# Expert outputs added into four sums in DRAM by POOL's scatter, in place of a pick per token and expert

## The reference, cut to what matters

```python
router_logits = x @ gate_w
probs = jax.nn.softmax(router_logits, axis=-1)
top_vals, top_idx = jax.lax.top_k(probs, 8)
top_vals = top_vals / jnp.sum(top_vals, axis=-1, keepdims=True)
rw = jnp.zeros((T, 64)).at[jnp.arange(T)[:, None], top_idx].set(top_vals)
h = silu(x @ w_gate[e]) * (x @ w_up[e]) * rw[:, e]     # for each expert e
out = sum over e of h @ w_down[e]
x = x + tanh(g_ffn[1]) * out                           # x is normalised before the experts
```

## Time and profile before

| what | value |
|---|---|
| median of three runs | 416.84 us (415.79 to 417.10) |
| the profiled execution | 417.87 us |
| its span | 416.1 us |
| mean granted TensorE clock | 0.844 |
| PE / PEld busy | 275.1 / 230.9 us |
| DVE / ACT / POOL busy | 210.7 / 118.0 / 214.0 us |
| bytes moved by DMA | 84.12 MB |

### The profile page before, as it was taken

The page is one execution under the profiler, slowest core; times in us unless marked ns, Lnnn a source line. Parts: engine busy times, 40 slices in busy tenths (PEclk is TensorE's granted clock), DMA queues, the critical chain, the costliest instruction groups (busy, mean ns, idle before and its releaser), DMA issues.

```text
span 416.1 us, 5526 instructions
## 1 busy us (share of the span) xinstructions
PE 275.1 (66%) x1546; PEld 230.9 (55%) x1546; DVE 210.7 (51%) x921; ACT 118.0 (28%) x265; POOL 214.0 (51%) x256
## 2 busy tenths in 40 slices
PE   5898177137801610000199999999999999951997
PEld 1335067037800500000189999889999889931886
DVE  0799999989386679000033433343433343340352
ACT  2264353316634500000023333333333333320000
POOL 2622112013267777777327777777777777771000
PEclk9999999557975555555589999999999999995899
DMA  4899995360013333333498888888888887226891
GB/s 132 312 352 306 318 310 192 91 190 2 1 63 113 126 126 127 126 127 138 148 243 267 273 270 277 271 264 274 261 273 269 269 270 229 74 73 234 325 305 64
DMA packets 47374, 84.12 MB, mean 202 GB/s; under 512 B 10453, under 2 KB 28249, under 8 KB 46320
## 3 DMA queue, kind: packets, MB, share of 16 engines
q1 hardware_dynamic: 38128, 64.87, 49.9%
q0 software_dynamic: 9216, 18.90, 13.0%
HBM read 48.07 MB, written 39.85 MB: 211 GB/s over the span
## 4 chain that ended last, share of the span: by engine, by line
PE 52%; DVE 18%; POOL 16%; issue 7%; DMA 4%; ACT 2%; SPq 1%; POOLq 1%; ACTq 0%
PE psum L715 20%; POOL expert_rows L478 14%; PE psum L724 13%; PE psum L770 7%; PE psum L704 5%; DVE work L995 5%; DVE top L991 5%; DVE stats L966 2%; PE psum L536 2%; PE psum L530 2%; DMA sim<-token_picks 1%; POOL token_picks L499 1%; PE psum L604 1%; DVE adj L1000 1%; DMA gu_w<-expert_rows 1%
## 5 line engine op out<-in xcount | busy, mean ns | idle before, releaser
L499 POOL DMA_INDIRECT token_picks<-down_w,target x126 | 117.3, 931 | 54.9 <-issue 41.1
L715 PE MATMUL psum<-gu_w,wgu 128*96 128x192 f32 x504 | 93.7, 329 | 0.0
L715 PEld LDWEIGHTS psum<-gu_w,wgu 128*96 128x96 f32 x504 | 78.0, 165 | 0.6 <-DVE gu_w L1203 0.2
L478 POOL DMA_INDIRECT expert_rows<-x_rows,place_at x64 | 62.4, 975 | 23.8 <-issue 23.8
L724 PE MATMUL psum<-proj_t,gu_w 96*96 96x256 f32 x252 | 64.8, 379 | 0.0
L927 ACT ACTIVATE gu_w<-psum 96x192 f32<-96x192 f32 x63 | 20.6, 326 | 130.0 <-PE psum L715 130.0
L1208 DVE TENSOR_TENSOR gu_w<-gu_w,psum 96x192 f32<-96x192 f32 x63 | 22.1, 350 | 67.1 <-ACT gu_w L927 67.1
L704 PE MATMUL psum<-ident,gu_w 96*128 96x96 f32 x108 | 14.1, 256 | 53.1 <-DMA gu_w<-expert_rows 53.1
L933 ACT COPY down_w<-psum 96x512 f32<-96x512 f32 x63 | 36.6, 581 | 33.9 <-PE psum L724 33.9
L724 PEld LDWEIGHTS psum<-proj_t,gu_w 96*96 96x96 f32 x252 | 41.1, 163 | 7.1 <-DVE gu_w L1208 0.4
L704 PEld LDWEIGHTS psum<-ident,gu_w 96*128 96x128 f32 x108 | 12.5, 148 | 57.6 <-DMA gu_w<-expert_rows 54.4
(11 more groups left out here) (177 smaller groups left out, 397.1 us busy)
## 6 DMA issues: line engine op xcount, KB each, us to landing
expert_rows<-empty_rows SPq DMA_DIRECT2D x1, 15360.0 KB, 69.3
wgu<-in_L_ffn_w_gate_up SPq DMA_DIRECT2D x65, 192.0 KB, 2.9
gu_w<-expert_rows SPq DMA_DIRECT2D x28, 240.0 KB, 4.2
proj_t<-in_L_ffn_w_down SPq DMA_DIRECT2D x65, 96.0 KB, 4.0
sim<-expert_rows SPq DMA_DIRECT2D x18, 240.0 KB, 4.3
work<-expert_rows SPq DMA_DIRECT2D x18, 240.0 KB, 4.2
gu_w<-in_L_ffn_gate_up_proj SPq DMA_DIRECT2D x4, 512.0 KB, 8.2
sim<-token_picks SPq DMA_DIRECT2D x2, 1024.0 KB, 4.9
```

The costliest lines, as they stand in the source:

```text
L478: pool.indirect_dma_start(rows_dram, bass.IndirectOffsetOnAxis(ap=place_at[:, t, k:k + 1], axis=0), x_rows[:, t, :], None).then_inc(placed ...
L499: pool.indirect_dma_start(picks_dram, bass.IndirectOffsetOnAxis(ap=target[0:SLOTS, e % T_RING, i:i + 1], axis=0), y_slots[0:SLOTS, n, i, : ...
L715: last = pe.matmul(psum[0:I1, 2 + e % 2, part * CAP:(part + 1) * CAP], wgu[:, n, k, part * I1:(part + 1) * I1], x_slots_t[:, e % 2, k, :], ...
```

## The change

- token_picks is gone. There are four DRAM tensors token_sums0 to 3, each of 1024 rows for the tokens and 192 spare rows, cleared by SP with four more DMAs (1.25 MB each) behind the clearing of expert_rows.
- A row of expert_rows is 256 features, one integer and 64 router weights: 321 words instead of 320. The integer is the token's number, the same for all experts; a cleared row has the number of a spare row and weights of zero.
- VectorE copies an expert's column of weights (slot_w) beside the target rows. ACT takes y out of PSUM with two activations per unit, each scaled by slot_w, instead of one copy.
- POOL's scatter adds (compute_op=ALU.add) to the sum of ring slot e % 4. No row is skipped; slots without a token are added to spare rows.
- order, pick_weights, build_diag and the diagonals are gone. router_weights runs before place_rows for each batch, POOL's placements wait for it, and ACT computes the exponentials of batches 0 and 1 earlier, after a table load that now stands before copy_logits(0).
- At the end SP loads each sum in two halves of 0.5 MB as soon as its last scatter has landed, and TensorE adds the four sums with 4 matmuls a tile with ident.
- X_RING is 9 instead of 10. POOL writes two more small constants by iota.

```diff
-X_RING = 10
+X_RING = 9
-    ROW = D + NE
+    ROW = D + 1 + NE
-    picks_dram = nc.dram_tensor("token_picks", [T * TOP_K_EXPERTS, D], F32, kind="Internal").ap()
+    sums_dram = [nc.dram_tensor(f"token_sums{n}", [T + CAP, D], F32, kind="Internal").ap() for n in range(Y_RING)]
...
+            for n in range(Y_RING):
+                sp.dma_start(sums_dram[n].rearrange("(r p) d -> p r d", p=CLEAR_P),
+                             empty_rows[0:CLEAR_P, 0:1, 0:D].to_broadcast([CLEAR_P, (T + CAP) // CLEAR_P, D])).then_inc(sums_cleared, 16)
...
             for n in range(Y_RING):
-                if n != LAST_Y:
+                if n == LAST_Y:
+                    sp.wait_ge(scattered[n], total_over * (16 * SUBS) + SCATTERED[n])
+                    sp.sem_inc(over_begun, 1)
+                else:
                     sp.wait_ge(scattered[n], SCATTERED[n])
-            picks_f = picks_dram.rearrange("(t p k) d -> t p (k d)", p=P, k=TOP_K_EXPERTS)
-            for t in range(NT):
-                need(sp, picks_summed, t - K_RING + 1)
-                sp.dma_start(picks[t % K_RING], picks_f[t]).then_inc(picks_landed[t % K_RING], 16)
+                for half in range(2):
+                    tiles = slice(half * NT // 2, (half + 1) * NT // 2)
+                    sp.dma_start(sums[n][:, tiles], sums_dram[n][0:T].rearrange("(t p) d -> p t d", p=P)[:, tiles]).then_inc(sums_landed[half][n], 16)
...
                         pool.wait_ge(place_ready, b + 1)
+                        pool.wait_ge(rw_ready, b + 1)
...
+            pool.wait_ge(sums_cleared, 16 * Y_RING)
             def scatter(e):
                 n = e % Y_RING
                 pool.wait_ge(y_ready, e + 1)
                 for i in range(SUBS):
-                    pool.indirect_dma_start(picks_dram, bass.IndirectOffsetOnAxis(ap=target[0:SLOTS, e % T_RING, i:i + 1], axis=0),
-                                            y_slots[0:SLOTS, n, i, :], None, bounds_check=T * TOP_K_EXPERTS - 1, oob_is_err=False).then_inc(scattered[n], 16)
+                    pool.indirect_dma_start(sums_dram[n], bass.IndirectOffsetOnAxis(ap=target[0:SLOTS, e % T_RING, i:i + 1], axis=0),
+                                            y_slots[0:SLOTS, n, i, :], None, bounds_check=T + CAP - 1, oob_is_err=True, compute_op=ALU.add).then_inc(scattered[n], 16)
...
-            for t in range(NT):
-                pe.wait_ge(diag_ready, t + 1)
-                pe.wait_ge(picks_landed[t % K_RING], 16 * (t // K_RING + 1))
-                for k in range(TOP_K_EXPERTS):
-                    last = pe.matmul(psum[:, t, 0:D], diag[:, t % 2, k, :], picks[t % K_RING][:, k * D:(k + 1) * D],
-                                     start=k == 0, stop=k == TOP_K_EXPERTS - 1)
-                last.then_inc(picks_summed, 1)
+            for half in range(2):
+                for n in range(Y_RING):
+                    pe.wait_ge(sums_landed[half][n], 16)
+                for t in range(half * NT // 2, (half + 1) * NT // 2):
+                    for n in range(Y_RING):
+                        last = pe.matmul(psum[:, t, 0:D], ident[:], sums[n][:, t], start=n == 0, stop=n == Y_RING - 1)
+                    last.then_inc(tokens_summed, 1)
...
+            act.preload_act_table(ACT.Exp)
             copy_logits(0)
             copy_logits(1)
+            exp_logits(0)
+            exp_logits(1)
             evacuate_down(2 * NE0 - 2)
             evacuate_down(2 * NE0 - 1)
-            act.preload_act_table(ACT.Exp)
-            exp_logits(0)
-            exp_logits(1)
...
-                act.copy(y_slots[0:SLOTS, n].rearrange("p i d -> p (i d)"), psum[0:SLOTS, 4 + e % 2, 0:SUBS * D]).then_inc(y_ready, 1)
+                for i in range(SUBS):
+                    last = act.activation(y_slots[0:SLOTS, n, i], psum[0:SLOTS, 4 + e % 2, i * D:(i + 1) * D], ACT.Copy,
+                                          scale=slot_w[0:SLOTS, e % T_RING, i:i + 1])
+                last.then_inc(y_ready, 1)
...
             choose_experts(1)
+            router_weights(0)
             place_rows(0)
+            router_weights(1)
             place_rows(1)
...
             choose_experts(2)
-            router_weights(0)
+            choose_experts(3)
+            router_weights(2)
             place_rows(2)
-            choose_experts(3)
-            router_weights(1)
+            router_weights(3)
             place_rows(3)
...
-            router_weights(2)
-            router_weights(3)
-            for b in range(B):
-                pick_weights(b)
...
-                dve.tensor_copy(target[0:SLOTS, e % T_RING], x_slots[e % X_RING][0:SLOTS, :, D + e + 1].bitcast(U32))
+                dve.tensor_copy(target[0:SLOTS, e % T_RING], x_slots[e % X_RING][0:SLOTS, :, D].bitcast(U32))
+                dve.tensor_copy(slot_w[0:SLOTS, e % T_RING], x_slots[e % X_RING][0:SLOTS, :, D + e + 2])
```

More of the change, by code:

```diff
@@ L163, in gated_layers_kernel @@
         reuse = gu_w[:].rearrange("p e k n -> p (e k n)")
-        cuts = [0, 4 * SUBS * ROW]
+        cuts = [0, 3 * SUBS * ROW]
         for n in (2 * KC * CAP, 2 * CAP, 2 * CAP):
             cuts.append(cuts[-1] + n)
-        x_homes = [(reuse, n) for n in range(4)]
+        x_homes = [(reuse, n) for n in range(3)]
         for home in (sim, work):
@@ L177, in gated_layers_kernel @@
         y_slots = down_w[:].rearrange("p e i d -> p (e i d)").rearrange("p (n i d) -> p n i d", n=Y_RING, i=SUBS)
-        diag = xn_t[:].rearrange("p k t -> p (k t)").rearrange("p (n k j) -> p n k j", n=2, k=TOP_K_EXPERTS)
-        picks = [t[:].rearrange("p t s -> p (t s)") for t in (sim, work, adj, base)]
+        sums = [t[:].rearrange("p t s -> p (t s)").rearrange("p (t d) -> p t d", d=D) for t in (sim, work, adj, base)]
         psum = stack.enter_context(nc.psum_tensor("psum", [P, N_BANKS, BANK], F32))
@@ L209, in gated_layers_kernel @@
         over_begun = sem("over_begun")
-        picks_landed = [sem(f"picks_landed{n}") for n in range(K_RING)]
-        diag_ready, picks_summed = sem("diag_ready"), sem("picks_summed")
+        sums_cleared = sem("sums_cleared")
+        sums_landed = [[sem(f"sums_landed{half}_{n}") for n in range(Y_RING)] for half in range(2)]
+        tokens_summed = sem("tokens_summed")
         out_ready, stored = sem("out_ready"), sem("stored")
@@ L946, in _ @@
                 act.wait_ge(scattered[LAST_Y], j * (16 * SUBS) + SCATTERED[LAST_Y])
-                act.copy(y_slots[0:SLOTS, LAST_Y].rearrange("p i d -> p (i d)"), psum[0:SLOTS, 4 + LAST_TWO, 0:SUBS * D]).then_inc(y_ready, 1)
+                for i in range(SUBS):
+                    last = act.activation(y_slots[0:SLOTS, LAST_Y, i], psum[0:SLOTS, 4 + LAST_TWO, i * D:(i + 1) * D], ACT.Copy,
+                                          scale=over_w[0:SLOTS, i:i + 1])
+                last.then_inc(y_ready, 1)
         @block.vector
@@ L1077, in place_rows @@
                 dve.wait_ge(chosen_ready, b + 1)
-                dve.wait_ge(consts_ready, 9)
-                for t in tiles:
-                    last = dve.tensor_tensor_scan(order[:, t], chosen[:, t], zeros[:], 0.0, ALU.add, ALU.add)
-                link(last)
-                for t in tiles:
-                    dve.tensor_scalar(x_rows[:, t, D:ROW].bitcast(U32), order[:, t], -1.0, token_end[:, t:t + 1], ALU.mult, ALU.add)
+                dve.wait_ge(consts_ready, 10)
                 filled(F_RANK[b])
@@ L1104, in router_weights @@
                 link(dve.tensor_scalar(e_scale[:, both], e_scale[:, both], tg[:, 3:4], None, ALU.mult))
-                dve.tensor_tensor(rw[:, both], e_val[:, both], e_scale[:, both].rearrange("p (t a) -> p t a", a=1).to_broadcast([P, HB, NE]),
+                dve.tensor_tensor(x_rows[:, both, D + 1:ROW], e_val[:, both], e_scale[:, both].rearrange("p (t a) -> p t a", a=1).to_broadcast([P, HB, NE]),
                                   ALU.mult).then_inc(rw_ready, 1)
-            def pick_weights(b):
-                dve.wait_ge(rw_ready, b + 1)
-                for t in tiles_of(b):
-                    for k in range(TOP_K_EXPERTS):
-                        last = dve.scalar_tensor_tensor(out=picked[:, t % 4, k], in0=order[:, t], scalar=float(TOP_K_EXPERTS - k), in1=rw[:, t],
-                                                        op0=ALU.is_equal, op1=ALU.mult, accum_out=pick_w[:, t, k:k + 1])
-                link(last)
             keep_top(1)
@@ L1185, in _ @@
             for i in range(SUBS):
[L1186 removed]
+                last = dve.tensor_scalar(over_void[:, i], bank(F_OVER)[:, 2 * P:3 * P], slot_row[:, i:i + 1], spare_row[:, i:i + 1], ALU.is_le, ALU.mult)
             last.then_inc(evac["dve"], 1)
@@ L1208, in up_times_silu1 @@
                 dve.tensor_tensor(h1_t[:, e % 2], silu1[:, e % 2], psum[0:I1, 2 + e % 2, CAP:2 * CAP], ALU.mult).then_inc(h_ready, 1)
-            def build_diag(t):
-                need(dve, picks_summed, t - 1)
-                for k in range(TOP_K_EXPERTS):
```

(2 more changed lines are left out.)

43 lines of the change are left out of this document (20 added, 23 removed).

## The result

The changed kernel takes **468.9 us** (467.99 to 470.39) where the kernel before, timed beside it, takes 416.97: a ratio of 1.125, 95% interval 1.121 to 1.129. The forecast was 412, with a range of 400 to 433. The profiled execution has a span of 467.3 us, 51.2 more than before.

The account below looks back on a forecast made before the run. TensorE was taken to bound the expert stage at 2.50 us an expert, POOL close behind. 417.87 - 14.9 + 2.0 + 5.0 + 2.0 + 1.0 = 413.0, less 1.0 for the profiled run: 412 us, range 400 to 433.

Parts of the forecast that it names:

- last scatter's issue to first closing matmul: Kernel's end: last load 1.2 us shorter at some 3.8 us, last scatter's landing up to 1 us longer.
- closing matmuls and what follows: TensorE's end: 32 matmuls instead of 64, 16.8 us instead of 30.5, so 13.7 us less.
- POOL's issue: Expert stage: adding scatter takes 0.07 us more, an expert 2.58 us; 5.0 us lost, bounds 0 and 21.
- rival (b): Expert stage: POOL becomes the bound and the kernel slower, from 0.11 us more per scatter; 428 at 0.20 more; chance 0.20.
- The engines: DMA in expert stage: added row counts as two moves, backlog mostly absorbed by the loads' lead; +2 us, bounds 0 and 8.
- rival (d): Expert stage: an adding row costs the DMA engines three moves or more, some 45 us more, 450; chance 0.07.
- The Trainium skill's rule on unaligned rows: Loads of x: 2568-byte rows need 11 or 12 transactions instead of 10; some 5 us of backlog, in no sum.
- rival (c): Expert stage: ACT's copy waits for late landings in the four y slots, binding above 7.06 us; 431; chance 0.15.
- ACT and VectorE: Expert stage: ACT's two scaled copies +0.35 us, VectorE's extra copy like 0.165; both hidden, scatter starts 0.3 us later once.
- The front: Start: POOL's first placement waits for router weights and starts later; +2.0 us, bounds 0.5 and 3.5.
- The end: After the expert stage: fewer matmuls save 13.7 us, smaller loads 1.2; 14.9 saved, before 1 us for the landing.

Follow-up runs that it names:

- e3_half_rows: Changed kernel with the second of each expert's two adding scatters covering 48 of its 96 rows; 465.36 us in one run.
- e4_one_add: Changed kernel with only the first of each expert's two adding scatters, wait counts halved; 409.04 us, ratio 0.982 to the kernel before.
- e2_skip: Changed kernel, still adding, with rows of empty slots skipped by the bounds check again; 468.57 us, ratio 1.125 to the kernel before.
- e7_wide_row_again: Repeat on e4_one_add with sums twice as wide: one scatter per expert adds 96 rows of 2 KB; 412.0 us, kernel before 479.11 beside it.
- e1_plain: Changed kernel with the addition removed from both scatters, all 192 rows of an expert still written; 410.21 us, ratio 0.985 to the kernel before.
- e5_late_loads: Changed kernel with the loads of all four sums put behind the last scatter's landing, first halves first; 467.23 us, ratio 1.120 to the kernel before.

## Why the prediction was wrong, point by point

Spans; the working is in the prediction.

| step | predicted | measured |
|---|---|---|
| first expert's rows asked for | +2.0 | +1.1 (203.41 to 204.55) |
| from there to the first scatter | +0.3, in no sum | +1.4 |
| first to last scatter (POOL 5.0, engines 2.0) | +7.0 | **+57.0** |
| last scatter's issue to first closing matmul | -0.2 | +5.75 |
| closing matmuls and what follows | -13.7 | -14.1 |
| sum | -4.9 | +51.1 |

**The step that failed is POOL's issue.** The prediction took 0.07 us more for an adding scatter, with an upper bound of about 0.20; it is 0.49 (1.407 against 0.915 to 0.922). The expert then needs 2 x 1.71 = 3.42 us and 63 x 0.92 = 58 us are lost, not 5. The slack of 0.06 us, the two scatters to an expert and the 0.30 us between were right, as was rival (b)'s mechanism and its point of decision at 0.11 us. Its size was wrong because the price was thought of as a price per row. e3_half_rows confirms the row's price at 1.4 ns, and shows that the addition's share isn't in it. Scaling that share by rows gave an upper bound that bounded nothing. Why the instruction costs so much more with the operand no run shows. The range and the chance of 0.20 for (b) followed from that bound.

**The engines.** The added row was taken as 92 ns, twice the plain one; it is 125 in the changed kernel, 110 in e4_one_add (0.264 x 50 x 16 / 1924 rows), 132 in e2_skip (0.312 x 50 x 16 / 1895), and 92 for each KB in 2 KB rows (0.444 x 50 x 16 us for 3838 KB). The Trainium skill, page Collectives: The Full Stack, section The bandwidth ceiling, has half the rate for an add: by that rule 92, which the wide rows agree with and the 1 KB rows exceed. At POOL's pace the cost in time is nothing, inside the bounds 0 to 8 us: e2_skip takes the share from 0.98 to 0.85 and gains nothing, and e7_wide_row_again runs the stage at TensorE's pace with all the bytes. So rival (d) isn't what took the time, though 125 ns is nearly the three moves it asked for: at POOL's 3.42 us an expert they fit, and in 2 KB rows, at two moves, all the bytes fit at 2.50. Whether 1 KB additions at 125 ns would fit at 2.50 (1.81 + 192 x 0.125/16 = 3.31 us of engine time by shares) no run shows. The Trainium skill's rule on unaligned rows, named in the prediction (page DMA: Bandwidth & Descriptors, section How a descriptor splits into AXI transactions), would take a tenth more for the x loads of 2568 bytes (11 transactions for 10; the prediction's 12 can't come up, as each piece starts at a multiple of 8 bytes); e1_plain's loads had 70.2% for 10.83 MB where the earlier trace rows have 72.5% for 10.80 MB, so nothing of it shows in the share of all loads.

**The ring**, rival (c): binding above 7.06 us of landing. The median is 5.0 us, and e4_one_add with 4.9 us runs at 2.50 us an expert. So the ring isn't the bound, despite 129 us of waits that bear its name.

**ACT and VectorE** were right: two activations take 0.83 us where the copy took 0.58, +0.25 for +0.35, and in e1_plain, which has them too, the stage from the first to the last scatter (216.8 to 376.32, 159.5 us) is no longer than the 160.6 of before.

**The front** was right in its mechanism and 0.9 us too high: the variance's L443 starts at 120.28 us where L439 started at 119.18, and the table load came before the logits' copies, as foreseen. From the asking for the first expert's rows to the first scatter 1.4 us came on top, for the 0.3 foreseen. In e1_plain, with the same instructions, it is 0.2 (205.04 to 216.77), and the difference is mostly TensorE's clock: in 212 to 215 us it was granted 0.66 here and 0.96 there, and 8 matmuls of L722 took 2.14 us for 1.47. That differs from run to run and is no part of the mechanism. The rows of the front:
```profile
109.89 1.28 ACT L906 ACT_TABLE_LOAD   x1
...
116.97 1.25 POOL L483 DMA_INDIRECT expert_rows<-x_rows,place_at  x1 [6.30 <-DVE place_at L1100]
...
120.28 0.72 POOL L443 TENSOR_TENSOR rstd<-var_eps,minus_half 128x2 f32<-128x2 f32 x1 [0.77 <-DVE var_eps L985]
```

**The end.** The matmuls were right to 0.4 us: 64 records for 128, 16.36 us for 30.50, with the first of them at the low clock again (0.58 in 448 to 454 us, then 1.00). The loads were not. The prediction had sums 0 to 2 loaded at no cost under the last expert and 0.5 MB to wait for; the early loads delay the scatter that the last sum waits for by some 3.5 us (6.72 against 3.25 in e5_late_loads), and the last load took 6.29, not 3.8. Of 13.9 us (14.9 less 1.0 for the landing) 8.4 arrived; e1_plain shows 9.2 (376.32 to 407.7 is 31.4).

So the gain of the end was really there, some 8 to 9 us, and e1_plain's ratio of 0.985 is what it is worth. It was bought with an operand that adds half to the price of POOL's scatter: 126 x 0.49 = 62 us of POOL's time, of which 4 had cover (63 x 0.06).

## What to carry to other kernels

Before an edit adds work to an engine that issues DMAs, work out its slack per period, and if the operation appears in no row, treat the price of the instruction as open: a bound made by scaling the known one by rows or bytes isn't a bound. Where such an operation has a fixed price per DMA, fewer and wider ones carry the same bytes: with 2 KB rows the stage ran at TensorE's pace again, though no working kernel was made of that. A wait's name isn't its cause; see whether the engine that is waited for was itself idle or at work throughout.

## What the runs showed of the hardware

- An indirect DMA that adds costs POOL 1.407 us to issue for 96 rows of 1 KB or of 2 KB, a plain one 0.915 to 0.922. Each row is 1.4 ns (48 rows: 1.339); the price doesn't follow the packets that the DMA makes, and rows dropped by the bounds check cost as much as moved ones.
- An added row of 1 KB takes 110 to 132 ns of a DMA engine, a plain one 46; in rows of 2 KB the addition takes 92 ns per KB. The recorded share reaches 1.09 with TensorE still at its pace, so a share of 1.0 alone does not show that the engines bind.
- With 3 MB of loads issued around it (in the changed kernel 2 MB ahead and 1 MB behind) the last scatter landed after 6.5 to 7.4 us (the changed kernel and e1 to e4), with the loads behind it after 3.25 (e5_late_loads).
- The kernel before took 480 us beside four runs and 417 beside the rest, once each on the same chip. Traces from beside the 480 us have waits, of 45 to 57 us ahead of the expert stage, whose source they can't name. That stays open.
